# Attention on one core: four key tiles of value products in each visit, in every second step

## The reference

```python
attn = jnp.einsum('bhqd,bhkd->bhqk', q, k) * scale
attn = jax.nn.softmax(attn, axis=-1)
out = jnp.einsum('bhqk,bhkd->bhqd', attn, v)
```

## Time and profile before

| what | value |
|---|---|
| median of three runs | 4760.73 us (4760.52 to 4762.82) |
| the profiled execution | 4758.41 us, its span 4756.6 us |
| PE busy over the span | 4643.6 us (98%) |
| POOL, DVE, ACT busy over the span | 3219.2, 3152.0, 2397.4 us |
| granted TensorE clock, mean | 0.985 |

### The profile page before, as it was taken

One profiled execution on the slowest core, in us unless ns is written; L12 is line 12 of the kernel. 1 busy time (PEld: TensorE's weight loads), 2 busy tenths in 40 slices (PEclk: granted clock), 3 DMA queues, 4 the chain that ended last, 5 costly groups with the idle time before them and its releaser, 6 DMA issues. The chain is left out here.

```text
span 4756.6 us, 66549 instructions
## 1 busy us (share of the span) xinstructions
PE 4643.6 (98%) x24396; PEld 2966.5 (62%) x24396; DVE 3152.0 (66%) x5296; ACT 2397.4 (50%) x4653; POOL 3219.2 (68%) x1117
## 2 busy tenths in 40 slices
PE   8999999999989999999999999999999999999969
PEld 6887878878845555555555555555555555555447
DVE  4323232333178888888888888888888888888534
ACT  2112121121126666666666666666666666666621
POOL 1121212122249999999999999999999999999920
PEclk9999999999979999999999999999999999999989
DMA  5334342434245656656566665666656666565476
GB/s 168 111 115 135 101 147 81 135 118 131 71 111 126 139 131 137 135 130 138 131 136 134 134 138 130 138 133 135 135 131 138 132 136 134 130 138 123 92 230 236
DMA packets 261849, 633.51 MB, mean 133 GB/s; under 512 B 46741, under 2 KB 80533, under 8 KB 222617
## 3 DMA queue, kind: packets, MB, share of 16 engines
q0 software_dynamic: 36864, 268.45, 27.8%
q1 hardware_dynamic: 224664, 360.85, 26.7%
HBM read 224.96 MB, written 134.74 MB: 76 GB/s over the span
## 5 line engine op out<-in xcount | busy, mean ns | idle before, releaser
L946 DVE TENSOR_REDUCE unit_max<-mx_ps 128x1 f32<-128x512 f32 x4096 | 2501.8, 680 | 323.1 <-PE mx_ps L1021 320.9
L855 POOL TENSOR_TENSOR p_pair<-p_sb 128x2048 f32<-128x2048 f32 x512 | 2471.6, 4875 | 57.2 <-ACT p_sb L932 53.6
L932 ACT ACTIVATE p_sb<-st_ps 128x512 f32<-128x512 f32 x4096 | 2062.1, 628 | 863.0 <-PE st_ps L1092 862.8
L1092 PE MATMUL st_ps<-q_x,k_x 97*128 97x512 f32 x4096 | 1592.8, 410 | 3.4 <-ACT p_sb L932 2.5
L1021 PE MATMUL mx_ps<-k_x,q_x 96*128 96x512 f32 x4096 | 1573.2, 407 | 22.0 <-DMA k_x<-k_lo_d 20.0
L1092 PEld LDWEIGHTS st_ps<-q_x,k_x 97*128 97x128 f32 x4096 | 734.7, 189 | 537.3 <-issue 380.0
L1033 PE MATMUL o_ps<-p_sb,v_sb 128*32 128x512 f32 x8192 | 989.7, 601 | 0.0
L1021 PEld LDWEIGHTS mx_ps<-k_x,q_x 96*128 96x128 f32 x4096 | 782.8, 191 | 299.8 <-DVE unit_max L946 109.9
L285 POOL TENSOR_TENSOR h_lo<-h_f,h_hi 128x512 fp32r<-128x512 f32 x128 | 165.1, 1291 | 693.3 <-DVE h_hi L469 693.3
L1033 PEld LDWEIGHTS o_ps<-p_sb,v_sb 128*32 128x32 f32 x8192 | 214.1, 109 | 434.1 <-issue 280.8
L469 DVE CAST h_hi<-h_f 128x512 fp32r<-128x512 f32 x128 | 55.0, 431 | 543.5 <-ACT h_f L342 543.5
(11 more groups left out here) (94 smaller groups left out, 3812.5 us busy)
## 6 DMA issues: line engine op xcount, KB each, us to landing
p_pair<-p_pair POOLq DMA_DIRECT2D x256, 1024.0 KB, 7.5
q_x<-q_hi_d SPq DMA_DIRECT2D x128, 256.0 KB, 5.4
k_x<-k_hi_d SPq DMA_DIRECT2D x128, 256.0 KB, 3.9
xt<-x SPq DMA_DIRECT2D x64, 256.0 KB, 2.6
stage<-w SPq DMA_DIRECT2D x32, 512.0 KB, 5.0
q_hi_d<-qk_hi SPq DMA_DIRECT2D x64, 256.0 KB, 3.0
q_lo_d<-qk_lo SPq DMA_DIRECT2D x64, 256.0 KB, 3.8
k_hi_d<-qk_hi SPq DMA_DIRECT2D x64, 256.0 KB, 2.6
```

What stands on the lines that cost most here:

```text
L855: pool.tensor_tensor(p_pair[:, slot, :, :], p_sb[:, n % SLOTS, :, :], p_sb[:, (n + 1) % SLOTS, :, :], ALU.add).then_inc(pair_done, 1)
L932: act.activation(p_sb[:, (L * G * KT + n) % SLOTS, h, :], st_ps[bank(g, m)][:, :], ACT.Exp, scale=SCALE).then_inc(exp_done, 1)
L946: dve.reduce_max(unit_max[:, n // 4, n % 4:n % 4 + 1], mx_ps[UNIT_PLACE[n] % RING][:, :], AX.X).then_inc(bank_read, 1)
L1092: pe.matmul(st_ps[bank(g, m)][:, :], k_x[u][:, h, kt * P:(kt + 1) * P], q_x[qc][:, h, :], start=True, stop=True).then_inc(st_ready, 1)
```

## The change

The value products stand in every second step only (0, 2, 4 and 6), and each visit takes four key tiles instead of two. The first visit of a group takes the last four tiles of the group before. The waits for the loaded values and for the copied output move with the first tile, from step 1 to step 2.

The first part of the row sum moves from step 7 to step 6, behind the turn (`VTZ`). The second part stays in step 2 behind the values. The third part stays in step 3, where no values stand any more, so it is a short visit of its own. The number of U, S, T and Z in a group is the same, and so are all matmuls.

```diff
-    PARTS = [(2, 0, False, 7), (4, 0, True, 10), (0, NA, False, 11)]
+    PARTS = [(2, 0, False, 6), (4, 0, True, 10), (0, NA, False, 11)]
...
-        STEPS = ["USUSUSUVSSUSUUSUS", "USUSUSUVSSUSUUSUS", "USUSUSUVZSSUSUUSUS", "USUSUSUVZSSUSUUSUS",
-                 "USUSUSUVSSUSUUSUS", "USUSUSUVSSUSUUSUS", "USUSUSUVTSSUSUUSUS", "USUSUSUVZSSUSUUSUS"]
+        STEPS = ["USUSUSUVSSUSUUSUS", "USUSUSUSUSUSUSUS", "USUSUSUVZSSUSUUSUS", "USUSUSUZSSUSUUSUS",
+                 "USUSUSUVSSUSUUSUS", "USUSUSUSUSUSUSUS", "USUSUSUVTZSSUSUUSUS", "USUSUSUSUSUSUSUS"]
...
-                                    for kt in (KT - 2, KT - 1):
+                                    for kt in range(KT - 4, KT):
...
-                            if j == 1:
+                            if j == 2:
...
-                            for kt in (2 * j - 2, 2 * j - 1):
+                            for kt in range(2 * j - 4, 2 * j):
...
-                for kt in (KT - 2, KT - 1):
+                for kt in range(KT - 4, KT):
```

## The result

| kernel | median of four runs | ratio |
|---|---|---|
| before | 4760.62 us (4757.39 to 4762.82) | 1 |
| changed | 4932.07 us (4929.21 to 4935.36) | 1.036 (95% interval 1.0347 to 1.0372) |

The changed kernel is 3.6% slower, 171 us. The forecast was 4935 us. The profiled execution has a span of 4933.5 us, 176.9 more than the 4756.6 of before.

A forecast was written before the change was run, and what follows sets the result against it. PE sets the pace, with DVE at 0.599 us a unit behind four banks; per group 3.95 + 0.25 - 1.23 - 0.1 = +2.87 us, times 62.8, less 4, gives +176 and 4935 us, range 4890 to 4990 (chance 0.80).

The forecast's parts named there:

- Visits saved: Value visits: eight a group become four with values and one with sums alone, saving 3 x 0.41 = 1.23 us a group.
- The turn between values and sums: Step 6: PE goes from 32 columns to the turn and back, costing 0.25 us a group, bounds 0 and 0.41.
- Long stretches: Three stretches of 16 units between visits: PE waits for DVE to free banks, losing 1.09, 1.09 and 1.25 us.
- The cut stretch: Between the visits of steps 2 and 4, cut by the lone sum: 0.5 us a group lost.
- ACT: Exponentials, 0.50 us each against a score every 0.463: don't bind with scores at 0.60 in a stretch's second half; no charge.
- The early join and POOL: Step 6's sum needs the second join 4.3 us sooner; POOL runs ahead, so no charge, and -0.1 us a group.
- Rival B: Step 6: the early sum waits for its join in every group, 1.5 us a group, 5030 us; chance 0.08.
- The end: After the last turn: POOL's lead shortens the end by 4 us once; the last group otherwise takes about the same.
- The sum: Whole kernel: +2.87 us a group, 52.15 in place of 49.28, times 62.8 gives +180 us, less 4: +176.
- A: Stretches of 16 units: the saving counts and DVE keeps up, about -50 us, 4710 us; chance 0.06.
- D: Whole group: losses and savings cancel, 0.1 us a group, 6 us in all; chance 0.03.
- C: PE's clock in the attention stage drops to 0.95 from short stalls before most units, 5090 us in all; chance 0.03.

The follow-up runs named there:

- half reads: The changed kernel, but DVE reduces only 256 of the 512 columns of each unit: 4823.58 us; with the first sum part also back in step 7, 4720.05 us.
- the control: The kernel before, with DVE reducing only 256 of the 512 columns of each unit and the exponential's scale an eighth: 4725.2 us, 49.05 us a group.

## Why the prediction was right, point by point

**What bounds the kernel.** Right: PE by its turns, and DVE behind four banks as what PE waits for. The experiment with half reads and the sum in step 7 removes that wait, and 2.6 us a group go with it (51.54 to 48.96).

**Visits saved.** Forecast 3 x 0.41 = 1.23 us. In the distance of 5.83 us from which 0.41 was taken lies a wait of the eighth unit. In the control this wait is gone, and from visit to visit it is 5.78 us (2466.05 to 2471.83). So the price proper is about 0.37. The sum did not suffer, because the same wait was left out of what the long stretch costs: its visit comes 0.43 us behind the last unit (2485.28 to 2485.71) instead of 0.33.

**The turn between values and sums.** Forecast 0.25 with bounds of 0 and 0.41; measured 0.34. The reason given for going below the whole price, that half of it might be paid already, was wrong; the sentence on a whole change of mode was nearer.

**Long stretches.** Forecast 1.09, 1.09 and 1.25; unit 1 to unit 16 takes 7.76 us from 0 to 2 (1.05 more than PE's own) and 7.85 from 4 to 6 (2503.64 to 2511.49, 1.14). The rule "unit k waits for the read of unit k - 4" held to 0.04 us, for four banks, for three, and for reads of 448 columns. The reciprocal costs 0.1, not 0.16. DVE's pace was 0.599 us in the earlier trace rows too: 24 units take 14.35 us from the first to what follows them (1338.79 to 1353.14), so 0.598 each and not 0.58.

**The cut stretch.** Forecast 0.5, measured 0.43. The lone sum starts 0.52 us after the last unit ahead of it (2493.76 to 2494.28) instead of 0.40, as worked out.

**ACT.** Right for this kernel: it did not bind at 0.60 a score. It had less in hand than "doesn't bind" suggests, as the half reads show.

**The early join and POOL.** Right, and the most delicate of the steps. POOL ran ahead and the early sum found its join landed. POOL in the changed kernel, two joins and the wait between them:

```profile
2503.02 0.87 POOL L859 DMA_DIRECT2D p_pair<-p_pair  x1
2506.25 4.59 POOL L855 TENSOR_TENSOR p_pair<-p_sb 128x2048 f32<-128x2048 f32 x1 [2.36 <-ACT p_sb L932]
2511.13 0.88 POOL L859 DMA_DIRECT2D p_pair<-p_pair  x1 [0.30 <-POOL p_pair L855]
```

The sum at 2515.70 needs the join issued at 2503.02. The means follow the typical groups as forecast: 49.28 against 49.19 before, 52.07 against 52.09 after, so the -0.1 for groups that no longer wait came too. Rival B was given 0.08, and this is fair only for the kernel as a whole: at 50.6 us a group, with half reads, B comes true. The change stood some 1.5 us a group from it (52.07 against 50.59).

**The end.** Forecast 4 us less from the last turn to the end; measured 0.7 us more. The last group of the changed kernel:

```profile
4713.59 6.08 PE L1033 MATMUL o_ps<-p_sb,v_sb 128*32 128x512 f32 x32
...
4720.51 4.51 POOL L893 TENSOR_TENSOR p_pair<-p_pair 128x2048 f32<-128x2048 f32 x1
```

POOL's lead is there: its last addition starts 6.9 us after the last value visit, against 10.6 before (4533.16 to 4543.71), so nearly all of the 4 us came. The step that failed is another one: "The last group has no units and takes about the same." From the last turn to the last value visit it takes 63.5 us, against 59.4 before, and POOL can't finish before PE and ACT have made what it adds. From the last turn to the last addition it is 70.5 us, against 69.9. In this group the mean granted clock is 0.78 (4650 to 4720 us), where it was 0.89 before (4473.8 to 4543.7), and a visit of four tiles takes 5.3 to 6.1 us instead of 3.64. Why the clock is lower with merged visits was not tried.

**The sum.** Steady state: forecast 2.87 us a group, measured 52.07 - 49.28 = 2.79, which is 5 us less over 62 groups. The end: forecast -4, measured +0.7. The start: forecast about 0.8 of a group, 2.3 us, measured 3.6; of this 1.2 us lies ahead of the turn before it (1372.1 and 1373.3 us), where both kernels do the same work. These cancel to within a microsecond of the span (176.9 against 176), which is luck in the last digits. The mechanism and its size are shown; the fit to 3 us is not.

**The rivals.** A and D fell at the first row of DVE. C fell with the granted clock of 1.00: PE stands still for some 0.14 us before every unit of the second half of a stretch, and the clock stays at 2.4 GHz. A lower clock is seen elsewhere, in the last group (0.78) and behind a wait of 3.25 us for a join in the changed kernel with half reads. The Trainium skill, "TensorE: Matmul & The Clock Gate", under "A second HAM failure mode: psum-queue depth-cycling", tells of a kernel that cycles through its banks with short idles and whose clock swings. The steady groups of this trace do not show it, nor do those with three banks, where units stand 0.60 us apart in every step and the granted clock is 1.00 too.

**What stays open.** With half reads and the early sum, single joins last longer: one issued at 1999.93 us was still waited for at 2009.40, 9.5 us later, where the trace of before has 8.0. The median of all joins hardly moves, 7.8 us against 7.5 before and 7.9 in the changed kernel. Whether the long ones come from the phase against the key and query loads was not tried.

## What to carry to other kernels

When two engines share a ring of buffers and the faster one rests now and then, the length of the stretch between its rests matters, not the mean load: write down when buffer k is read and when it is filled again, with the two paces of the trace, and here the loss fell out to a few hundredths of a microsecond. Merging visits to save switches lengthens that stretch, so weigh 0.4 us saved against what the slower engine can't take. And after removing one wait look for what it covered: here the joins and ACT were each within some 3 us a group of being the bound.

## What the runs showed of the hardware that was not expected

- A change between 32-column and full-width work costs TensorE about 0.37 us there and back at 2.4 GHz, and a single small full-width product between two blocks of 32-column work costs nearly the same, 0.34 us.
- VectorE's maximum over a PSUM bank takes 0.599 us from start to start for 512 columns in float32, 0.53 for 448 and 0.33 for 256.
- ScalarE's exponentials of 512 columns start 0.49 us apart over 16 in a row (7.95 us), slower than the 0.463 at which TensorE makes a pair of products.
- TensorE's clock stayed at 1.00 with a stall ahead of most units, both in stretches of the changed kernel and in the steady groups with three banks. Behind one stall of 3.25 us it was 0.50 to 0.55 for some 3.5 us.
